# Second layer of a four-part model: other background steps, rates and row offsets around the state-space scan

## The reference, cut to what matters

```python
# x: (4, 2048, 256), float32
x = x + L0_attn(layernorm(x))        # RWKV-like recurrence and feed-forward
x = x + L0_ffn(layernorm(x))         # 2 shared and 16 routed experts
x = x + L1_attn(layernorm(x))        # the second layer's scan: the change lies around it
x = x + L1_ffn(layernorm(x))         # two groups of 32 experts, top 2 each

def L1_attn(x):                      # 512 inner channels, 16 states
    x_ssm, res = split(x @ W_in.T)
    x_ssm = silu(causal_conv4(x_ssm) + b_conv)
    B = (x_ssm @ W_x.T)[second half]
    dt = softplus(x_ssm @ W_dt.T + b_dt)
    h = exp(dt * A) * h + dt * B * x_ssm          # per time step, channel and state
    y = h.sum(states) + D * x_ssm
    return (y * silu(res)) @ W_out.T

def moe_group(x2):                   # in L1_ffn, twice
    scores = softmax(x2 @ router_w)
    weights, index = top_k(scores, 2)
    # tokens sorted by expert, SwiGLU per expert, weighted sum back
```

## Time and profile before

| what | value |
|---|---|
| median of 3 runs | 4982.31 us (4976.38 to 4983.9) |
| profiled execution, its own time | 4976.51 us |
| its span, first to last instruction | 4974.7 us |
| scan stage, from the first scan to the last | 2516.1 to 4282.9 us |
| busy share of the span: PE, DVE, POOL, ACT | 88%, 77%, 61%, 51% |

### The profile page before, as it was taken

The page is one execution under the profiler, slowest core; times in us unless marked ns, Lnnn a source line. Parts: engine busy times, 40 slices in busy tenths (PEclk is TensorE's granted clock), DMA queues, the critical chain, the costliest instruction groups (busy, mean ns, idle before and its releaser), DMA issues.

```text
span 4974.7 us, 58244 instructions
## 1 busy us (share of the span) xinstructions
PE 4357.1 (88%) x18832; PEld 2868.4 (58%) x18832; DVE 3827.0 (77%) x6152; ACT 2521.3 (51%) x4753; POOL 3045.1 (61%) x1956
## 2 busy tenths in 40 slices
PE   5789999999999999998988889998988888489994
PEld 1355555555555555565655655555555555378883
DVE  6897888878777887884168888888888888645677
ACT  1244333433433343333567777777777776245552
POOL 3455554545545455553167888888888888745552
PEclk7899999999999999999989999999999998699997
DMA  4233332333333233332121121112221111486787
GB/s 143 80 106 107 104 102 85 109 106 102 106 104 104 84 108 106 98 110 84 45 85 55 71 71 64 64 65 74 77 84 65 70 65 61 162 240 205 255 279 279
DMA packets 302509, 545.46 MB, mean 110 GB/s; under 512 B 30592, under 2 KB 146560, under 8 KB 293248
## 3 DMA queue, kind: packets, MB, share of 16 engines
q1 hardware_dynamic: 274560, 466.08, 29.0%
q0 software_dynamic: 27648, 75.67, 4.2%
HBM read 422.71 MB, written 118.92 MB: 109 GB/s over the span
## 4 chain that ended last, share of the span: by engine, by line
PE 59%; DVE 18%; ACT 10%; POOL 6%; issue 4%; DMA 2%; SPq 0%; DVEq 0%; another core or an unknown queue 0%; POOLq 0%; ACTq 0%
PE psum L207 23%; PE psum L783 8%; PE psum L1891 5%; DVE c_hs L1426 5%; PE psum L658 5%; POOL c_dbx L1408 4%; PE psum L1150 4%; PE psum L1442 3%; DVE a_S L885 3%; PE psum L1914 3%; PE psum L1198 3%; DVE a_prod L891 2%; PE psum L907 2%; ACT psum L1415 2%; PE psum L1876 1%
## 5 line engine op out<-in xcount | busy, mean ns | idle before, releaser
L1408 POOL TENSOR_TENSOR c_dbx<-c_dtx,c_Brep 128x1024 f32<-128x1024 f32 x512 | 1203.0, 2365 | 266.6 <-DVE c_hs L1426 211.3
L876 POOL TENSOR_TENSOR a_kv<-a_rk,a_kv 128x512 f32<-128x512 f32 x512 | 813.5, 1601 | 387.4 <-DMA a_kv<-v_rows 387.4
L1426 DVE TENSOR_TENSOR_SCAN c_hs<-psum,c_carry,c_dbx 128x512 f32<-128x512 f32 x768 | 934.8, 1264 | 148.7 <-ACT psum L1415 115.9
L802 POOL TENSOR_TENSOR a_hid_e<-a_hid_e,a_g_rep 128x512 f32<-128x512 f32 x256 | 386.8, 1513 | 823.8 <-ACT a_hid_e L791 646.9
L885 DVE TENSOR_TENSOR_SCAN a_S<-a_decay,a_carry,a_kv 128x513 f32<-128x513 f32 x512 | 792.0, 1547 | 103.0 <-POOL a_kv L876 99.0
L1415 ACT ACTIVATE psum<-c_dt,c_cols 128x512 f32<-128x512 f32 x1024 | 694.1, 687 | 296.7 <-DVE c_hs L1426 288.1
L1442 PE MATMUL psum<-ident,c_hs 128*128 128x128 f32 x4096 | 656.6, 299 | 152.8 <-DVE c_hs L1426 146.5
L1442 PEld LDWEIGHTS psum<-ident,c_hs 128*128 128x128 f32 x4096 | 521.7, 153 | 410.5 <-DVE c_hs L1426 239.8
L891 DVE TENSOR_TENSOR a_prod<-a_rk,a_S 128x512 f32<-128x512 f32 x512 | 580.9, 1135 | 78.8 <-PE psum L907 78.8
L783 PE MATMUL psum<-a_W_down,a_hid_e 128*128 128x256 f32 x2304 | 550.9, 385 | 62.1 <-DVE a_carry L883 35.5
L207 PE MATMUL psum<-a_xT,a_W_up 128*128 128x512 f32 x1152 | 561.1, 617 | 26.2 <-ACT a_hid_e L791 15.2
(11 more groups left out here) (263 smaller groups left out, 6890.9 us busy)
## 6 DMA issues: line engine op xcount, KB each, us to landing
a_kv<-v_rows SPq DMA_DIRECT2D x512, 256.0 KB
a_g_rep<-g_rows SPq DMA_DIRECT2D x256, 256.0 KB, 4.0
c_Brep<-b_rows SPq DMA_DIRECT2D x64, 1024.0 KB
d_xs<-sorted_rows SPq DMA_DIRECT2D x320, 128.5 KB
d_w<-results SPq DMA_DIRECT2D x64, 512.0 KB, 11.4
d_w<-in_d_experts SPq DMA_DIRECT2D x32, 768.0 KB
sorted_rows<-d_zeros SPq DMA_DIRECT2D x66, 128.5 KB, 11.3
a_xa<-in_L_attn_x SPq DMA_DIRECT2D x16, 512.0 KB, 4.6
```

The costliest lines, as they stand in the source:

```text
L876: m_kv[g] = pool.mark(nc.gpsimd.tensor_tensor(kv[:, g % NV, 1:C + 1], rk[slot][:, 1, hb, :], kv[:, g % NV, 1:C + 1], ALU.mult))
L1408: m_dbx[g] = m_dbx[g + 1] = pool.mark(nc.gpsimd.tensor_tensor(dbx[:, r:r + 2, :], dtx[slot][:, e, :].unsqueeze(1).broadcast_to([P, 2, C]), ...
L1426: m_scan[q] = dve.mark(nc.vector.tensor_tensor_scan(hs[:, q % NR, :], psum[:, DA + q % ND, :], dbx[:, q % NX, :], first, ALU.mult, ALU.add))
```

## The change

1. More background steps (`LAG` is 2): between conv and `c_xs` `LAG + 1` in place of 1; in `step_size` between PE and ACT `LAG + 1` in place of `LAG`; after W_out `LAG + 2` in place of `LAG + 1`; before the rank matmuls `LAG` in place of 1.
2. Rates: AFTER_RATE 1.15 to 1.2, BEFORE_RATE 1.15 to 1.3.
3. The gate product (now L1456) is issued at turn `g - AHEAD - 6` in place of `- 4`.
4. The start of each expert's room is added by a third rank matmul with one row of `route.room` (L1313), in place of DVE's `index * pitch` (L1344 before) and of the float copy of the index (L1538 before). Only in the last chunk DVE adds it.
5. The row number of each token is no longer written by DVE in each chunk (L1290 before): from chunk 2 on POOL adds a constant to the number that the buffer had two chunks ago (L1358).
6. The reciprocal of the weights' total goes to PSUM, and the weights are made from it in `router`.

```diff
-                yield
+                yield from pause(LAG + 1)
                 for e, i, bank, m in held:
                     act.after(m, *scanned)
...
                 m = pe.mark(m)
-                yield from pause(LAG)
+                yield from pause(LAG + 1)
                 act.after(m, *scanned, m_done.get(("tmp free", e % 2)))
...
-            yield from pause(LAG + 1)
+            yield from pause(LAG + 2)
             dve.engine.wait_ge(s_xb, c * 16 + 16)
...
             dve.after(m_xn)
-            dve.mark(nc.vector.tensor_scalar(xn_[:, :, D], token_row[:, :], float(c * C * TOP), None, ALU.add))
-            dve.after(m)
-            dve.mark(nc.vector.scalar_tensor_tensor(out=route.weights[:, part, :].rearrange("p t (g k) -> p (t g) k", g=GR), in0=R["best"][:, :, 0:TOP], scalar=0.5,
-                                                    in1=R["total"][:, :].unsqueeze(2).broadcast_to([P, TL * GR, TOP]), op0=ALU.mult, op1=ALU.mult))
-
+            if c < 2:
+                dve.mark(nc.vector.tensor_scalar(xn_[:, :, D], token_row[:, :], float(c * C * TOP), None, ALU.add))
...
-            yield
+            yield from pause(LAG)
             i, bank = yield from G.claim(pe)
...
+            if c < NCH - 1:
+
+                pairs.append((ones[0:1, :], route.room[0:1, :].unsqueeze(1).broadcast_to([1, TL, NE])))
+            m_rank = m_done["yT free", c] = pe.mark(matmuls(nc, ranks, pairs))
...
-            m = dve.mark(nc.vector.scalar_tensor_tensor(out=place[:, :, :, :].rearrange("p t g k -> p (t g) k"), in0=R["index_f"][:, :, :], scalar=float(Z.pitch),
-                                                        in1=place[:, :, :, :].rearrange("p t g k -> p (t g) k"), op0=ALU.mult, op1=ALU.add))
...
-            pool.after_alone(*m_done["placed", c])
+            m_row = None
+            if c >= 2:
+
+                pool.engine.wait_ge(s_sorted[c % 2], c // 2 * per_chunk)
+                m_row = pool.mark(nc.gpsimd.tensor_tensor(route.xn[c % 2][:, :, D], route.xn[c % 2][:, :, D], two_chunks[:, :], ALU.add))
+            pool.after_alone(*m_done["placed", c], m_row)
...
-        AFTER_RATE, BEFORE_RATE, SORT_RATE, AHEAD = 1.15, 1.15, 0.4, 2
+        AFTER_RATE, BEFORE_RATE, SORT_RATE, AHEAD = 1.2, 1.3, 0.4, 2
...
-            for g in range(total + AHEAD + 4):
+            for g in range(total + AHEAD + 6):
...
-                q = g - AHEAD - 4
+                q = g - AHEAD - 6
...
-    dve.mark(nc.vector.tensor_copy(R["index_f"][:, :, :], R["index"][:, :, 0:top]))
-    dve.mark(nc.vector.reciprocal(R["total"][:, :], R["total"][:, :]))
+    per_total = bank[:, TL * NE + rows * top:TL * NE + rows * (top + 1)]
+    m_total = dve.mark(nc.vector.reciprocal(per_total, R["total"][:, :]))
+    dve.after(m_total)
+    dve.mark(nc.vector.scalar_tensor_tensor(out=weights, in0=best[:, :, 0:top], scalar=0.5, in1=per_total.unsqueeze(2).broadcast_to([P, rows, top]), op0=ALU.mult, op1=ALU.mult))
```

More of the change, by code:

```diff
@@ L1285, in after_scan @@
             pe.after(*marks)
-            m = yield from router(nc, L, G, yT, W_router, R, iota, GR, EX, TOP, LAG)
+            weights = route.weights[:, c * TL:(c + 1) * TL, :].rearrange("p t (g k) -> p (t g) k", g=GR)
+            m = yield from router(nc, L, G, yT, W_router, R, iota, weights, GR, EX, TOP, LAG)
             chosen = R["chosen"][:, :, :].rearrange("p (t g) e -> p t (g e)", t=TL)
-            part = slice(c * TL, (c + 1) * TL)
             dve.after(m_xn)
-            dve.mark(nc.vector.tensor_scalar(xn_[:, :, D], token_row[:, :], float(c * C * TOP), None, ALU.add))
-            dve.after(m)
-            dve.mark(nc.vector.scalar_tensor_tensor(out=route.weights[:, part, :].rearrange("p t (g k) -> p (t g) k", g=GR), in0=R["best"][:, :, 0:TOP], scalar=0.5,
-                                                    in1=R["total"][:, :].unsqueeze(2).broadcast_to([P, TL * GR, TOP]), op0=ALU.mult, op1=ALU.mult))
+            if c < 2:
+                dve.mark(nc.vector.tensor_scalar(xn_[:, :, D], token_row[:, :], float(c * C * TOP), None, ALU.add))
             ahead = route.ahead
@@ L1309, in after_scan @@
                 m_all = pe.mark(matmuls(nc, counts[:, 0:NE], [(ones[:, :], ahead[:, TL, :])]))
-            m_rank = m_done["yT free", c] = pe.mark(matmuls(nc, ranks, [(tri[:, :], R["chosen"][:, :, :].rearrange("p r e -> p (r e)")),
-                                                                       (ones[:, :], ahead[:, 0:TL, :].rearrange("p t e -> p (t e)"))]))
+            pairs = [(tri[:, :], R["chosen"][:, :, :].rearrange("p r e -> p (r e)")), (ones[:, :], ahead[:, 0:TL, :].rearrange("p t e -> p (t e)"))]
+            if c < NCH - 1:
+                pairs.append((ones[0:1, :], route.room[0:1, :].unsqueeze(1).broadcast_to([1, TL, NE])))
+            m_rank = m_done["yT free", c] = pe.mark(matmuls(nc, ranks, pairs))
             yield from pause(LAG)
@@ L1335, in after_scan @@
                 dve.after(m)
+                m = dve.mark(nc.vector.tensor_tensor(moved, moved, route.room[:, :].unsqueeze(1).broadcast_to([P, TL, NE]), ALU.add))
+                dve.after(m)
                 ranks = moved.rearrange("p t e -> p (t e)")
@@ L1473, in layer1_phase @@
         W_out, W_router, iota = sb("W_out", [P, EB, D]), sb("W_router", [P, KB, NE]), sb("iota", [P, 32])
-        token_row = sb("token_row", [P, TL])
+        token_row, two_chunks = sb("token_row", [P, TL]), sb("two_chunks", [P, TL])
         xb, yT = sb("xb", [P, TL, D]), sb("yT", [P, EB, C])
@@ L1490, in layer1_phase @@
         dve.mark(nc.vector.memset(ones[:, :], 1.0))
+        dve.mark(nc.vector.memset(two_chunks[:, :], float(2 * C * TOP - (TOP - 1))))
         scanned_out = scans()
@@ L1494, in layer1_phase, with router @@
         route.scanned = scanned_out
-def router(nc, L, G, xT, W_router, R, iota, groups, experts, top, lag=1):
+def router(nc, L, G, xT, W_router, R, iota, weights, groups, experts, top, lag=1):
     TL, KB = 4, 2
```

## The result

The changed kernel takes 5017.95 us (median of 4 runs, 5015.7 to 5022.76) against 4983.1 for the kernel before on the same chip: ratio 1.0074, 95% interval 1.0062 to 1.0086. It is slower, by about the amount that was forecast (5011). Its profiled execution is the longest of the four, 5022.76 us. These are its page's span and its busy time by stretch, to be read against the earlier trace rows: chunks 1 to 11, 14 and 15.

The account below looks back on a forecast made before the run. No single engine bounds a chunk: PE is full in its first part, DVE in its second. Chunks 1 to 11 +22, chunks 12 to 15 to +19, drain +10: +29 on 4976.5, raised by 5.8, 5011 us; range 4930 to 5040.

Parts of the forecast that it names:

- The router's place, +4.0 a chunk: Chunks 1 to 11: router moves from behind 36 scans to behind 44, where DVE has no gap; +4.0 us a chunk.
- waits for exponentials "unchanged near 10 us a chunk": Sign for chunks 1 to 11: DVE's waits for ACT's exponentials at the first part stay near 10 us a chunk.
- The pauses, -0.5: More background steps: DVE's waits for `c_tmp`, 0.85 us a chunk, shrink by 0.5; nothing gained before `c_xs`.
- So 0 for `c_xs`: Behind conv: with PE full, an exponential issued sooner feeds scans whose transposes queue behind the same matmuls; gain 0.
- L1538, L1344, L1290, -1.8: Three small instructions removed from DVE: 0.7, 0.1 and 1.0 us gained a chunk.
- the rank matmul, +0.3: Third rank matmul on PE, in the chain on which DVE's `c_at_pick` waits: +0.3 us a chunk.
- the near 1.1 us named as a sign: Sign: L1294, the copy of the counts, grows from 0.18 us to a mean near 1.1.
- The rule on the shared port pair: DVE and GpSimd lock shared ports per instruction; alone it has the counts' copy inherit L1290's wait, term -0.1, forecast 10 higher.
- Chunks 12 to 15, -3: Last chunks: chunk 12 +2 for the router's place, chunks 13 and 14 -2 each, chunk 15 -1 us.
- The drain, +10: After the last scan: 20 DMA instructions and two additions in POOL's queue delay chunk 15's `c_rstd` root; +10 us.
- slower still: Rival: counts' copy inherits L1290's wait, another small instruction L1538's; +3.8 us a chunk, 5037 us, chance 0.15.
- ACT frees DVE: Rival: added steps remove DVE's waits for exponentials, 2.5 to 5 us a chunk; 4922 to 4957 us, chance 0.30.

Follow-up runs that it names:

- gate_back: Changed kernel with the gate product back at turn g - AHEAD - 4, router behind 36 scans: 4963.8 us, 0.9964 of the kernel before.
- late_router9: gate_back with nine idle steps just ahead of the router, the rest of after_scan kept early: 5028.9 us, 1.0089 of the kernel before.
- late_after6: gate_back with six idle steps at the start of after_scan, router behind 44 scans: 5036.3 us, 1.0130 of the kernel before.
- order_only: Kernel before with only the changed kernel's pauses, rates and gate turn, old operations kept: 5030.8 us, 1.0101 of the kernel before.
- bank_early: Changed kernel whose router frees its PSUM bank after subtracting the peak, index and total's reciprocal in SBUF: 5026.6 us, 1.0093 of the kernel before.
- ops_only: Changed kernel with pauses, rates and gate turn of the kernel before, only the edited operations left: 4979.8 us, 0.9994 of the kernel before.
- gate_only: Kernel before with only the gate product moved to turn g - AHEAD - 6: 4998.0 us, 1.0022 of the kernel before.

## Why the prediction was right, and where it was not

The direction came out as forecast, and so did the two places of the loss, chunks 1 to 11 and the drain. The size did so partly by luck. Between the traces chunks 1 to 11 lost 40.6 us, where +22 was forecast, and chunks 12 to 15 gained 13.0, where a gain of 3 was forecast; the drain's 11 us were forecast as 10. Term by term, for chunks 1 to 11:

- **The router's place, +4.0 a chunk.** It is the cause, shown by gate_back, late_router9 and late_after6, and mis-sized: with the pauses and rates in, two turns of the gate cost 115.2 - 109.4 = +5.7. The net of all order edits was forecast as 4.0 - 0.5 = 3.5 and is 3.9 (order_only, 115.4 - 111.5). The mechanism was right: the router's work lies where DVE has nothing to spare, and the part that it left still takes what PE needs (the table of the parts). DVE's idle time there grew with it. So what was named as a sign, waits for exponentials "unchanged near 10 us a chunk", contradicts the mechanism and was wrong: they are 14.1. How far the router's bank, held longer, adds to the 5.7 is open, up to 2.5 (bank_early).
- **The pauses, -0.5.** Mis-sized: pauses and rates bring -1.9 (gate_back against ops_only). The step that failed is the argument behind "So 0 for `c_xs`", that an exponential issued sooner gains nothing where PE is full. PE was busy through all of ACT's waits before `c_xs`, yet these fell from 48.4 us (ops_only) to 28.3, those before `c_tmp` from 45.0 to 10.1, and DVE's waits for exponentials by 46.5. No run has one pause or one rate alone, so how the 1.9 divides between `c_xs`, `c_tmp` and the rates is open.
- **L1538, L1344, L1290, -1.8, and the rank matmul, +0.3.** Together -1.5 was forecast. At the old places it is 0 (ops_only). In the new order it is -0.3 a chunk between profiles and 0.3% between ratios (1.0074 against 1.0101). The instructions' time did go: L1294 takes 195 ns, not the near 1.1 us named as a sign. But DVE waits for the rank matmuls before `c_at_pick` 27.5 us in place of order_only's 13.1, so what DVE saved was partly given back to PE. The +0.3 was low as well: the third product (`route_room`) is two instructions of 448 ns a chunk, 0.9 us on PE.
- **The rule on the shared port pair** would have made the forecast 10 us higher. It names the right thing, the common ends, and in ops_only the copy inherits the wait as the rule has it. That a place beside POOL's product decides, and not the instruction, is what the runs add: in the changed kernel no instruction inherits it.
- **Chunks 12 to 15, -3.** Measured -13. The sum had no term for router work that leaves these chunks; chunk 14 lost 5.9 us and chunk 15 6.3, and a part of this work is what PE and DVE do in the drain.
- **The drain, +10.** Measured 11.1. POOL's queue was as described, 20 DMA instructions and two additions, though its wait for landing was 1.66 us and not 4.7, and one DMA instruction was issued only after 2.25 us. It was not alone: the transposes of chunk 15 began at 4318.97, behind chunk 14's rank matmuls on PE, so that ACT was ready for the root only 2.8 us before POOL was. Of ACT's delay 2 us are W_out's matmuls at the lower clock. Freeing POOL's queue alone would have given back 2.8 us, by that reading. This was not tried.

Along the kernels before, ops_only, gate_back, changed the errors a chunk were +1.7 (place), -1.4 (pauses) and +1.4 (operations: -0.1 in ops_only for -1.5), so two of them cancelled, and the +1.7 left, some 19 us in eleven chunks, was offset by the 10 us of chunks 12 to 15; the rest is scatter between profiles and medians (46 us between the profiles, 35 between the medians). The range held the result with room, but the closeness of 5011 to 5018 is in part luck. Of the rivals, "slower still" had the right chunk length (+3.8) by another sum, and "ACT frees DVE" a real mechanism that lost to the place.

## What to carry to other kernels

When two engines are full in turn, ask of each background step in which of the two stretches it lies: here eight scans' delay of the router, out of PE's full stretch, cost 5.7 us a chunk, while DVE's total work fell. An edit that delays the source of a stream (here the gate product, two turns) shifts everything behind it, and by more than its own delay (three scans in gate_only, eight here); raise the stream's rate with it. And test an order edit and an operation edit apart: here the order edits together cost 1.0%, the operations alone gained nothing, and in between lay a version 0.4% faster.

## What the runs showed of the hardware

Some small DVE instructions beside a running GpSimd product were stretched to the product's end: copies and casts within SBUF (1.86 us for the copy of the counts in ops_only) and products of two inputs in SBUF (2.26 us for the weights' product in bank_early). The weights' product was not stretched when one of its inputs lay in PSUM (0.17 us, issued 0.12 us after the product began). Lying in SBUF is not enough. In the changed kernel the sum over `c_prob`, with its input in SBUF, takes 0.39 us and ends well inside the product, and the statistics of `c_xb` take 409 ns in the mean beside a product and 413 apart from one. Chunk 5, DVE, then POOL:

```profile
3147.63 0.39 DVE L1529 TENSOR_REDUCE c_total<-c_prob 128x8 f32<-128x256 f32 x1
...
3146.62 2.37 POOL L1412 TENSOR_TENSOR c_dbx<-c_dtx,c_Brep 128x1024 f32<-128x1024 f32 x1 [6.55 <-DVE c_hs L1430]
```

The Trainium skill (page "SBUF — State Buffer", section "SBUF: two separate sides") has the lock taken by DVE instructions in a 2-port mode or with two inputs from SBUF. The trace agrees for the weights' product, which has two such inputs in bank_early and one in the changed kernel. The copy has one input, as the sum has that was not stretched, so its wait needs the first half of that rule. In which mode an instruction ran, no trace here shows.
